# Graph-by-graph products in the hypergraph layer of a four-layer graph network, and attention masks on two row groups of the array

## The chip, the cores and the metric

The kernel runs on one core of a Trainium2 chip. The metric is the device time of one execution in microseconds (us), the median over several runs; lower is better.

## What is computed

128 graphs of 64 nodes with 256 features pass through four layers, each followed by a residual sum and a layer normalisation. The change touches the first (attention with masks) and the third (hypergraph convolution), cut here to what matters:

```
# layer 0, 8 heads of 64
dots = jnp.where(m2, einsum('bhid,bhjd->bhij', q, k) * scale, -big)      # m2: mask of row node and mask of column node
attn = softmax(dots) * LA + LG * adj + LD * jnp.exp(-dist)
# layer 2, twice (256 -> 512 with relu and a norm, then 512 -> 256)
H   = (adj != 0)                                   # 64 x 64 per graph
Dn  = 1 / einsum('nce,ne->nc', H, adj[:, 0])       # 0 where the sum is 0
Be  = 1 / H.sum(axis=1)
m   = Be[:, :, None] * einsum('nce,nch->neh', H, x @ W.T)
out = Dn[:, :, None] * einsum('nce,neh->nch', H, m) + b
```

With G = Dn H Be H^T the layer is G (x W^T) = (G x) W^T. G is a 64 x 64 matrix per graph.

## The kernel before

A group is eight graphs, 512 nodes, held as four tiles (T = 4) of 128 nodes: two graphs to a tile, nodes on the partitions. There are 16 groups. In each round of the main loop four streams work on four different groups: N (split and projections of the newest group), A (attention), B (the mean layer and the hypergraph layer) and D (the last layer). The order in which each engine walks through the steps of a round is a list written out by hand (`PE_ORDER`, `ACT_ORDER`, `DVE_ORDER`, `POOL_ORDER`); the change leaves the four lists as they are. Every engine works strictly through its list and waits on counting semaphores. The 16 groups overlap, so that the last groups run in rounds in which streams are missing.

PSUM has eight banks of 128 x 512 float32. Streams N and A use banks 0 to 3 in turn, B and D banks 4 to 7, so the bank of a step is given by its place in `PE_ORDER`; `filled` and `emptied` count when a bank is full and when its earlier reader is done. `apart` adds an increment of a semaphore that nobody waits for between two waits.

Steps that the text speaks of:

- `mixmat` and `score` (stream A). The mask of the node pairs is added by TensorE itself: a product of two small factors with 4 rows, `mi` (4 x 128 per tile) and `mj` (4 x 64 per tile), in bfloat16. `score` first writes it into the banks `s_even` and `s_odd` with four products of 256 columns (L1083), then adds 32 products of queries and keys on squares of 64 x 64 (L1093). There are two `score` steps in a round.
- `graph_c`: S = (H^T scaled by Be) times H^T into bank `sym`, four products 128 x 128 (L1182), float32. A tile holds two graphs, so H^T is two 64 x 64 squares on the diagonal and zeros elsewhere. VectorE multiplies the bank by `dn` into `gmat` (L890). `graph_d` transposes it (L1190) and ScalarE copies it to `gT`.
- `spread`: the feature gather G x, transposed: features on the partitions, nodes on the columns. Step 0 is features 0 to 127 into one bank, step 1 features 128 to 255 into the next, four products 128 x 128 each (L1201). ScalarE rounds each bank to `spT_hi` (L578), VectorE writes the rest to `spT_lo` (L709).
- `v` 2: six products of 512 columns for attention values, the step between `spread` 1 and `up` 0 in `PE_ORDER`.
- `up` 0 to 3: W1 times the gathered features, six products of 512 columns each (L1022 to L1024), the first three on feature chunk 0 and the next three on chunk 1.
- `pv` (L1128) fills two banks `oT` at once with 32 products on 64 x 64 squares; ScalarE copies both (L601), VectorE subtracts (L709), and `out0` (L1022, `wo_hi`) reads the result.
- `sim` (L1284): products of 128 rows and 64 columns. `stat` (L1248): four products with one moving column.

A float32 product appears in the trace as two passes, each with a weight load of its own; a product of `_hi`/`_lo` operands or of bfloat16 appears as one.

Of the kernel before, what the change touches and what calls it, by code (L numbers as in the profile page):

```python
# [12 lines left out]
ALU = mybir.AluOpType  # L13
ACT = mybir.ActivationFunctionType
# [18 lines left out]
HC = HID // P  # L33
NBIAS = D
EPS_LN = 1e-5
MIX = 0.33
# [100 lines left out]
def graph_layers(nc, x, x_t, adj, adj_t, adj_row0, mask_rows, wqkv, w_out, b_out, w_mean_t, w1_t, b1_c, gamma_c, beta_c, w2_t, b2,  # L137
                 wqk_t, bqk_c, wl_t, bl, wr_t, wd_r, bd_r, ident_c, ones3_c, mrow_c, out):
    with ExitStack() as ctx:
# [38 lines left out]
        warm = sb("warm", [P, T])  # L178
        mcst = sb("mcst", [4, 1 + P])

        masks = sb("masks", [4, T * (P + N)], U8)
        mi = sb("mi", [4, T, P], BF16)
        mj = sb("mj", [4, T, N], BF16)
        xTin = sb("xTin", [P, C, TOK])
# [98 lines left out]
        def count(sem, g, k, back=0):  # L283


            n = g * PER[sem] + (k - back * PER[sem])
            return (zero_ready, 6) if isinstance(n, int) and n <= 0 else (SEM[sem], n)

        def apart(eng, g):
# [259 lines left out]
        def _(act):  # L549
# [71 lines left out]
            def up(g, i):  # L621
                if isinstance(g, int) and g == 0 and i == 0:
                    act.wait_ge(bias_in, 16 * 8)
                copy_out(g, "up", i, r[:, i, :], "relu_ready", ACT.Relu, bias=b1c[:, i:i + 1])

            def hid_hi(g, i):
                act.wait_ge(*count("relu_ready", g, i + 1))
                if i == C:
                    apart(act, g)
                    act.wait_ge(*filled("qk", C - 1, g, 1))  # L630
                    apart(act, g)
                    act.wait_ge(*filled("y3", T - 1, g, 1))
                act.activation(hT[0][:, i, :], r[:, i, :], ACT.Copy).then_inc(SEM["hT_hi"], 1)  # L633
# [18 lines left out]
            def qk(g, i):  # L652
# [10 lines left out]
                "graph_d": lambda g, i: copy_out(g, "gT", 0, flat(gT[:, :, :]), "gT_ready"),  # L663
                "spread": lambda g, i: copy_out(g, "spread", i, spT[0][:, i, :], "spread_hi"),
                "hid_hi": hid_hi, "sq": sq, "mean_h": mean_h,
# [6 lines left out]
        def _(dve):  # L672
# [117 lines left out]
            def mask(g, i):  # L790

                dve.wait_ge(*count("mask_in", g, 16))
                dve.scalar_tensor_tensor(out=mi[:, :, :], in0=masks[:, 0:T * P].rearrange("p (t n) -> p t n", n=P),
                                         scalar=mcst[:, 0:1], in1=mcst[:, 1:1 + P].rearrange("p (a n) -> p a n", a=1)
                                         .broadcast_to([4, T, P]), op0=ALU.max, op1=ALU.mult)\
                   .then_inc(SEM["mask_rows"], 1)
                dve.tensor_scalar(flat(mj[:, :, :]), masks[:, T * P:T * (P + N)], mcst[:, 0:1], None,
                                  ALU.max).then_inc(SEM["mask_rows"], 1)
                if isinstance(g, int) and g == 0:
                    other_weights(0)  # L800
# [84 lines left out]
            def graph_c(g, i):  # L885

                dve.wait_ge(*filled("sym", 0, g))
                src = bank_of("sym", 0)
                dve.wait_ge(*count("dn_ready", g, 1))
                ins = dve.tensor_tensor(gmat[:, :, :], src[:, :].rearrange("p (t n) -> p t n", t=T),  # L890
                                        wide(dn[:, :], P), ALU.mult)
                ins.then_inc(SEM["g_ready"], 1)

            def agg(g, i):

                lo, hi = 2 * i, 2 * i + 2
                dve.wait_ge(*filled("agg", i, g))
                src = bank_of("agg", i)
                dve.wait_ge(*count("rdeg_ready", g, 1))
                for k in range(2):  # L900
                    ins = dve.scalar_tensor_tensor(out=xl[1][:, lo + k, :], in0=src[:, k * D:(k + 1) * D],
                                                   scalar=rdeg[:, lo + k:lo + k + 1], in1=xl[1][:, lo + k, :],
                                                   op0=ALU.mult, op1=ALU.add)
                ins.then_inc(SEM["agg_out"], 1)
                dve.wait_ge(*count("agg_out", g, i + 1))
                apart(dve, g)
                dve.wait_ge(*count("x1_ready", g, 2))

                ins = dve.scalar_tensor_tensor(out=flat(xl[1][:, lo:hi, :]), in0=flat(xl[1][:, lo:hi, :]), scalar=0.0,
                                               in1=flat(xl[0][:, lo:hi, :]), op0=ALU.max, op1=ALU.add)  # L910
                ins.then_inc(SEM["sum1_ready"], 1)
                dve.wait_ge(*count("sum1_ready", g, i + 1))
                norm(g, 1, xl[1], lo, hi)

            def hid_lo(g, i):
# [61 lines left out]
            def agg3(g, i):  # L977
# [29 lines left out]
                "turn1": low_chunk(x1T, "turn1", "turn1"),  # L1007
                "spread": low_chunk(spT, "spread", "spread"),
                "turn3": low_chunk(xgT, "turn3", "turn3"),
# [4 lines left out]
        def _(pe):  # L1014
# [19 lines left out]
            def mixmat(g, i):  # L1034
# [4 lines left out]
                for t in range(T):  # L1039
                    ins = pe.matmul(dst[:, t * N:(t + 1) * N], mi[:, t, :], mj[:, t, :],  # L1040
                                    start=True, stop=True)
# [28 lines left out]
            def score(g, i):  # L1070
# [9 lines left out]
                apart(pe, g)  # L1080
                for e in range(2):
                    for k in range(2):
                        pe.matmul(dst[e][:, k * HP * N:(k + 1) * HP * N], mi[:, 2 * i + k, :],  # L1083
                                  mj[:, 2 * i + k:2 * i + k + 1, :].broadcast_to([4, HP, N]),
                                  start=(k == 0), stop=False, skip_group_check=True)
# [91 lines left out]
            def graph_c(g, i):  # L1177
                pe.wait_ge(*count("bht_ready", g, 1))
                pe.wait_ge(*emptied("sym", 0, g))
                dst = bank_of("sym", 0)  # L1180
                for t in range(T):
                    ins = pe.matmul(dst[:, t * P:(t + 1) * P], hT0[:, t, :], bhT[:, t, :], start=True, stop=True)  # L1182
                now_full(ins, "sym", 0)

            def graph_d(g, i):
# [5 lines left out]
                now_full(ins, "gT", 0)  # L1191

            def gathered(name, g, i, src, mat, halves=None):


                pe.wait_ge(*emptied(name, i, g))
                dst = bank_of(name, i)
                for t in range(T):
                    if halves and i == 0 and t % 2 == 0:
                        pe.wait_ge(*count(halves, g, t // 2 + 1))  # L1200
                    ins = pe.matmul(dst[:, t * P:(t + 1) * P], src[:, t, i * P:(i + 1) * P], mat[:, t, :],  # L1201
                                    start=True, stop=True)
                now_full(ins, name, i)

# [17 lines left out]

            def spread(g, i):
                pe.wait_ge(*count("gT_ready", g, 1))
                gathered("spread", g, i, xl[1], gT, "x2_ready")

            def up(g, i):
                if isinstance(g, int) and g == 0 and i == 0:
# [4 lines left out]
                now_full(product(dst[:, :], [(chunk(w1, c, slice(i * P, (i + 1) * P)), chunk(spT, c)) for c in range(C)],  # L1233
                                 [count("spread_lo", g, c + 1) for c in range(C)]), "up", i)

# [113 lines left out]
```

## Time and profile before

| | |
|---|---|
| median of 3 runs | 1185.15 us (1184.29 to 1186.23) |
| the profiled execution: time, span | 1184.85 us, 1182.8 us |
| mean granted TensorE clock | 0.986 |
| busy share of the span | TensorE 95%, its weight loads 80%, VectorE 78%, ScalarE 50%, GpSimd 48% |
| bytes moved | 31 GB/s over the span |

The engines are named PE (TensorE), PEld (its weight loads, which overlap PE), DVE (VectorE), ACT (ScalarE), POOL (GpSimd). The table gives shares of the whole span. Start times of successive passes tell what a pass costs in a stream; the duration shown for one pass holds its latency too and overlaps the next.

### The profile page before, as it was taken

What the parts mean: (1) busy time and instruction counts of PE and PEld (TensorE: products, weight loads), DVE (VectorE), ACT (ScalarE), POOL (GpSimd) and SP (SyncE); (2) the same over time, 40 slices, a digit from 0 to 9 for tenths busy, and PEclk for the clock granted to TensorE, in tenths of its full rate; (3) what the DMA queues carried; (4) which work ended last, traced back from release to release, by engine and by line L of the source; (5) the groups of instructions that cost most, each with busy time, mean ns of one, the idle gap of its engine ahead of it and who ended that gap; (6) DMA issues with size and microseconds to landing.
All of it is one profiled execution on the core that took longest, in us unless ns stands there. A gap on an engine that the chain in (4) does not pass through costs nothing.

```text
span 1182.8 us, 29171 instructions
## 1 busy us (share of the span) xinstructions
PE 1127.0 (95%) x10416; PEld 951.4 (80%) x10416; DVE 919.8 (78%) x2223; ACT 595.7 (50%) x1266; POOL 572.5 (48%) x731
## 2 busy tenths in 40 slices
PE   5889999999999999999999999999999999999875
PEld 4768888888888888888888888888888888888763
DVE  6675887878788887878877788788778878777865
ACT  2536465454646445474544647454464645546331
POOL 2426356382644628264472735537273553826341
PEclk9899999999999999999999999999999999999897
DMA  7010102010010201001020100102001010100000
GB/s 233 24 28 1 46 3 67 1 48 21 22 44 0 67 0 44 22 22 44 0 67 0 43 24 22 44 0 67 0 23 44 18 49 0 42 8 28 2 23 18
DMA packets 52868, 37.22 MB, mean 31 GB/s; under 512 B 28182, under 2 KB 47707, under 8 KB 52827
## 3 DMA queue, kind: packets, MB, share of 16 engines
q1 hardware_dynamic: 51272, 35.09, 9.7%
q10 hardware_dynamic: 1554, 1.58, 0.5%
q8 instruction: 26, 0.43, 0.1%
q14 instruction: 16, 0.12, 0.0%
HBM read 28.27 MB, written 8.39 MB: 31 GB/s over the span
## 4 chain that ended last, share of the span: by engine, by line
PE 90%; DVE 5%; ACT 2%; POOL 1%; issue 1%; DMA 0%; SPq 0%; POOLq 0%; DVEq 0%; ACTq 0%
PE bank L1022 22%; PE bank L1024 21%; PE bank L1023 20%; PE bank L1093 3%; PE bank L1128 3%; PE bank L1163 2%; PE bank L1220 2%; PE bank L1201 2%; PE bank L1106 2%; PE bank L1294 2%; PE bank L1258 2%; DVE oT_lo L709 2%; PE bank L1083 1%; PE bank L1284 1%; PE bank L1248 1%; PE bank L1182 1%
## 5 line engine op out<-in xcount | busy, mean ns | idle before, releaser
L529 POOL TENSOR_TENSOR prob<-prob,srec 128x512 f32<-128x512 f32 x64 | 71.6, 1118 | 146.9 <-DVE srec L832 146.9
L467 POOL TENSOR_SCALAR var<-mv 128x2 f32<-128x2 f32 x128 | 29.0, 227 | 208.6 <-DVE mv L779 208.6
L786 DVE TENSOR_SCALAR x<-x,mv,rstd 128x256 f32<-128x256 f32 x256 | 119.0, 522 | 3.8 <-POOL rstd L470 3.3
L590 ACT ACTIVATE v<-bank 64x256 f32<-64x256 f32 x256 | 96.7, 378 | 17.7 <-PE bank L1024 15.4
L477 POOL TENSOR_TENSOR bhT<-hT,be 128x512 f32<-128x512 f32 x16 | 18.3, 1144 | 168.3 <-PE bank L1172 168.3
L775 DVE BATCH_NORM_STATS2 stats<-x 128x6 f32<-128x256 f32 x256 | 96.4, 418 | 4.4
L470 POOL TENSOR_TENSOR rstd<-var,negh 128x2 f32<-128x2 f32 x128 | 91.1, 712 | 10.7
L534 POOL TENSOR_TENSOR prob<-prob,mix 128x512 f32<-128x512 f32 x64 | 86.7, 1355 | 6.0 <-POOL prob L529 1.9
L918 DVE TENSOR_TENSOR hT_lo<-r,hT_hi 128x512 fp32r<-128x512 f32 x64 | 69.7, 1089 | 22.4 <-ACT hT_hi L633 22.2
L1022 PE MATMUL bank<-wo_hi,oT_hi 128*128 128x256 f32 x256 | 75.1, 293 | 8.9 <-DVE oT_lo L709 8.9
L1022 PE MATMUL bank<-w_hi,hT_hi 128*128 128x258 f32 x256 | 75.8, 296 | 2.7 <-DVE hT_lo L918 2.1
L578 ACT ACTIVATE qT<-bank 128x512 f32<-128x512 f32 x64 | 38.4, 599 | 78.6 <-PE bank L1024 78.6
L578 ACT ACTIVATE yl<-bank 128x256 f32<-128x256 f32 x64 | 24.6, 385 | 105.7 <-PE bank L1024 105.3
L578 ACT ACTIVATE kT<-bank 128x512 f32<-128x512 f32 x64 | 38.2, 598 | 78.6 <-PE bank L1024 78.6
L490 POOL TENSOR_TENSOR r<-r 128x512 f32<-128x512 f32 x48 | 67.1, 1398 | 21.4 <-ACT r L638 18.4
L1024 PE MATMUL bank<-wo_hi,oT_lo 128*128 128x256 f32 x256 | 73.7, 288 | 0.0
L1023 PE MATMUL bank<-wo_lo,oT_hi 128*128 128x256 f32 x256 | 73.4, 287 | 0.0
L1023 PE MATMUL bank<-w_lo,hT_hi 128*128 128x258 f32 x256 | 72.4, 283 | 0.0
L1024 PE MATMUL bank<-w_hi,hT_lo 128*128 128x258 f32 x256 | 72.1, 282 | 0.0
L1022 PE MATMUL bank<-xT_hi,wk_hi 128*128 128x512 f32 x128 | 56.6, 442 | 13.7 <-DVE wk_lo L689 13.1
L578 ACT ACTIVATE pT<-bank 128x512 f32<-128x512 f32 x64 | 34.7, 595 | 59.1 <-PE bank L1106 59.1
L839 DVE TENSOR_TENSOR x<-bank,xin 128x512 f32<-128x512 f32 x32 | 22.1, 691 | 51.0 <-PE bank L1024 51.0
(202 smaller groups left out, 3697.9 us busy)
## 6 DMA issues: line engine op xcount, KB each, us to landing
xTin<-in_x_t SPq DMA_DIRECT2D x32, 256.0 KB, 2.8
xin<-in_x SPq DMA_DIRECT2D x16, 512.0 KB, 3.7
out_x<-x SPq DMA_DIRECT2D x32, 256.0 KB
adjA<-in_adj SPq DMA_DIRECT2D x16, 128.0 KB, 2.5
adjB<-in_adj_t SPq DMA_DIRECT2D x32, 64.0 KB, 3.1
adjC<-in_adj_t SPq DMA_DIRECT2D x32, 64.0 KB, 2.3
r<-in_wqkv ACTq DMA_DIRECT2D x2, 512.0 KB, 4.1
x<-in_wqkv SPq DMA_DIRECT2D x1, 512.0 KB, 8.2
```

The source lines that it names most:

```text
L470: pool.tensor_tensor(rstd[layer][:, lo:hi], var[layer][:, lo:hi], negh[:, lo:hi], ALU.pow).then_inc(SEM[f"rstd{n}"], 1)
L490: pool.tensor_tensor(r[:, 0, :], r[:, 0, :], r[:, i, :], ALU.add).then_inc(SEM["sqsum"], 1)
L529: pool.tensor_tensor(rows_of(u), rows_of(u), srec[:, k, :].rearrange("p (h a) -> p h a", a=1) .broadcast_to([P, 2 * HP, N]), ALU.mult).the ...
L534: pool.tensor_tensor(u, u, mix[:, t:t + 2, :].rearrange("p t (a n) -> p t a n", a=1) .broadcast_to([P, 2, HP, N]), ALU.add).then_inc(SEM[" ...
L578: act.activation(dst, src[:, part], func, **kw).then_inc(SEM[ready], 1)
L590: ins = act.activation(v[e * N:(e + 1) * N, i, gr, :, :], src[gr * N:(gr + 1) * N, e], ACT.Copy)
L775: dve.bn_stats(stats[layer][:, t, :], src[:, t, :]).then_inc(SEM[f"stats{n}"], 1)
L786: ins = dve.tensor_scalar(x[:, t, :], x[:, t, :], mv[layer][:, t, 0:1], rstd[layer][:, t:t + 1], ALU.subtract, ALU.mult)
L918: dve.tensor_tensor(hT[1][:, i, :], r[:, i, :], hT[0][:, i, :].bitcast(F32), ALU.subtract).then_inc(SEM["hT_lo"], 1)
L1022: pe.matmul(out_ap, l[0], rr[0], start=(fresh and j == 0), stop=False, skip_group_check=not fresh)
L1023: pe.matmul(out_ap, l[0], rr[1], start=False, stop=False, skip_group_check=not fresh)
L1024: ins = pe.matmul(out_ap, l[1], rr[0], start=False, stop=(last and j == len(pairs) - 1), skip_group_check=not fresh)
```

## The change

It has four parts. `graph_c` computes the two 64 x 64 squares of each tile alone (8 products on diagonal squares in place of 4), and VectorE scales the two squares in two operations. `spread` becomes one step: for each tile and each half of the features one product per graph, with the 64 nodes of the graph as rows, 128 features as weights and 64 moving columns; graph 0 of a tile goes to one bank, graph 1 to the other (16 products in place of 8). Each bank now holds both feature halves of four graphs, so ScalarE and VectorE read it contiguously and write it to every second stretch of 64 columns (`graph_of`), and `up` waits for both `spread_lo` before its first product. In `score` the mask factors lie on partitions 0 to 3 and again on 64 to 67; the products for `s_even` use the first copy, those for `s_odd` the second, and they alternate. The mask arrays therefore have 68 rows (MR) instead of 4.

```diff
+MR = N + 4
-        mcst = sb("mcst", [4, 1 + P])
-        masks = sb("masks", [4, T * (P + N)], U8)
-        mi = sb("mi", [4, T, P], BF16)
-        mj = sb("mj", [4, T, N], BF16)
+        mcst = sb("mcst", [MR, 1 + P])
+        masks = sb("masks", [MR, T * (P + N)], U8)
+        mi = sb("mi", [MR, T, P], BF16)
+        mj = sb("mj", [MR, T, N], BF16)
...
+        def graph_of(ap, h):
+            return ap[:, :, :].rearrange("p c (t a n) -> p c t a n", a=2, n=N)[:, :, :, h, :]
...
+            def spread(g, h):
+                act.wait_ge(*filled("spread", h, g))
+                act.activation(graph_of(spT[0], h), bank_of("spread", h)[:, :].rearrange("p (c t n) -> p c t n", c=C, t=T),
+                               ACT.Copy).then_inc(SEM["spread_hi"], 1)
...
-                ins = dve.tensor_tensor(gmat[:, :, :], src[:, :].rearrange("p (t n) -> p t n", t=T),
-                                        wide(dn[:, :], P), ALU.mult)
+                for h in range(2):
+                    at = slice(h * N, (h + 1) * N)
+                    ins = dve.tensor_tensor(gmat[at, :, at], src[at, :, at], wide(dn[at, :], N), ALU.mult)
...
+            def spread(g, h):
+                dve.wait_ge(*count("spread_hi", g, h + 1))
+                dve.tensor_tensor(graph_of(spT[1], h), bank_of("spread", h)[:, :].rearrange("p (c t n) -> p c t n", c=C, t=T),
+                                  graph_of(spT[0], h).bitcast(F32), ALU.subtract).then_inc(SEM["spread_lo"], 1)
...
-                for e in range(2):
-                    for k in range(2):
-                        pe.matmul(dst[e][:, k * HP * N:(k + 1) * HP * N], mi[:, 2 * i + k, :],
-                                  mj[:, 2 * i + k:2 * i + k + 1, :].broadcast_to([4, HP, N]),
+                for k in range(2):
+                    for e in range(2):
+                        rows = slice(e * N, e * N + 4)
+                        pe.matmul(dst[e][:, k * HP * N:(k + 1) * HP * N], mi[rows, 2 * i + k, :],
+                                  mj[rows, 2 * i + k:2 * i + k + 1, :].broadcast_to([4, HP, N]),
...
+                apart(pe, g)
                 for t in range(T):
-                    ins = pe.matmul(dst[:, t * P:(t + 1) * P], hT0[:, t, :], bhT[:, t, :], start=True, stop=True)
+                    for h in range(2):
+                        at = slice(h * N, (h + 1) * N)
+                        ins = pe.matmul(dst[at, t * P + h * N:t * P + (h + 1) * N], hT0[at, t, at], bhT[at, t, at],
+                                        start=True, stop=True, skip_group_check=True)
...
             def spread(g, i):
+                if i:
+                    return
                 pe.wait_ge(*count("gT_ready", g, 1))
-                gathered("spread", g, i, xl[1], gT, "x2_ready")
+                for h in range(2):
+                    pe.wait_ge(*emptied("spread", h, g))
+                    apart(pe, g)
+                ins = [None, None]
+                for t in range(T):
+                    if t % 2 == 0:
+                        pe.wait_ge(*count("x2_ready", g, t // 2 + 1))
+                        apart(pe, g)
+                    for c in range(C):
+                        for h in range(2):
+                            rows = slice(h * N, (h + 1) * N)
+                            col = (c * T + t) * N
+                            ins[h] = pe.matmul(bank_of("spread", h)[:, col:col + N], xl[1][rows, t, c * P:(c + 1) * P],
+                                               gT[rows, t, rows], start=True, stop=True, skip_group_check=True)
+                for h in range(2):
+                    now_full(ins[h], "spread", h)
...
-                                 [count("spread_lo", g, c + 1) for c in range(C)]), "up", i)
+                                 [count("spread_lo", g, C) for c in range(C)]), "up", i)
```

Where instructions stand on TensorE, at the gather. `gT,x` are the passes of `spread`, `wv` those of `v` 2, `yl,adjC` the last of stream D ahead of it. Before:

```order
L1294 MATMUL bank<-yl,adjC 128x257 [waits y3_ready,sim_ready]
L1201 MATMUL bank<-gT,x 128x128 [waits x2_ready,agg3_out,gT_ready]
L1201 MATMUL bank<-gT,x 128x128
L1201 MATMUL bank<-gT,x 128x128 [waits x2_ready]
L1201 MATMUL bank<-gT,x 128x128
L1201 MATMUL bank<-gT,x 128x128 [waits gT_ready]
L1201 MATMUL bank<-gT,x 128x128 x3
L1022 MATMUL bank<-wv_hi,xT_hi 128x512 [waits shift_ready]
```

Now, down to the first product of `up`:

```order
L1320 MATMUL bank<-yl,adjC 128x257 [waits y3_ready,sim_ready]
L1248 MATMUL bank<-gT,x 128x64 [waits gT_ready,x2_ready,agg3_out]
L1248 MATMUL bank<-gT,x 128x64 x7
L1248 MATMUL bank<-gT,x 128x64 [waits x2_ready]
L1248 MATMUL bank<-gT,x 128x64 x7
L1038 MATMUL bank<-wv_hi,xT_hi 128x512 [waits shift_ready]
L1039 MATMUL bank<-wv_lo,xT_hi 128x512
L1040 MATMUL bank<-wv_hi,xT_lo 128x512
L1038 MATMUL bank<-spT_hi,w_hi 128x512 [waits spread_lo,agg3_out]
```

Nothing has changed places with a step of another stream: eight products of 128 columns are sixteen of 64, the second bank is asked for at the start instead of in the middle, and the six products of `v` 2 still stand between the gather and `up` 0.

On VectorE, at `graph_c` of group 0, in a round ahead of the loop (the row `hT<-bank,dn` is the scaling of `sym` into `gmat`; the rows around it belong to the mean layer). Before:

```order
L775 BN_STATS stats<-x 128x6 [waits sum1_ready]
L775 BN_STATS stats<-x 128x6
L779 BN_AGGR mv<-stats 128x2 [waits stats1] x2
L890 TENSOR_TENSOR hT<-bank,dn 128x512 [waits dn_ready,bank4_full]
L901 SCALAR_TENSOR_TENSOR x<-bank,rdeg,x 128x256 [waits rdeg_ready,bank5_full]
L901 SCALAR_TENSOR_TENSOR x<-bank,rdeg,x 128x256
```

Now:

```order
L785 BN_STATS stats<-x 128x6 [waits sum1_ready]
L785 BN_STATS stats<-x 128x6
L789 BN_AGGR mv<-stats 128x2 [waits stats1] x2
L902 TENSOR_TENSOR hT<-bank,dn 64x4x64 [waits dn_ready,bank4_full]
L902 TENSOR_TENSOR hT<-bank,dn 64x4x64
L912 SCALAR_TENSOR_TENSOR x<-bank,rdeg,x 128x256 [waits rdeg_ready,bank5_full]
L912 SCALAR_TENSOR_TENSOR x<-bank,rdeg,x 128x256
```

The one operation over 128 partitions has become two over 64 partitions and half the columns, at the same place and behind the same waits.

## Rows read from the trace of the kernel before

**Rows 1.** The page: the chain that ended last, shares by engine.

```profile
PE 90%; DVE 5%; ACT 2%; POOL 1%; issue 1%; DMA 0%; SPq 0%; POOLq 0%; DVEq 0%; ACTq 0%
```

**Rows 2.** Windows, one round: length, busy time by engine (instructions), clock, DMA.

```profile
core 0: us, PE busy (x) PEld busy (x) DVE busy (x) ACT busy (x) POOL busy (x), PEclk, DMA share, GB/s
503.09:572.90 69.81, 69.37 (x652) 58.72 (x650) 56.11 (x137) 37.08 (x79) 35.80 (x45) 1.00 0.09 28
```

**Rows 3.** Timeline, PE, gather to `up` 0: start, us, line, passes.

```profile
508.05 1.95 PE L1201 MATMUL bank<-gT,x 128*128 128x128 f32 x16
509.75 0.47 PE L1022 MATMUL bank<-wv_hi,xT_hi 128*128 128x512 f32 x1
...
511.21 0.39 PE L1022 MATMUL bank<-spT_hi,w_hi 128*128 128x512 f32 x1
```

**Rows 4.** Timeline, ACT, the two copies of the gather.

```profile
509.13 0.60 ACT L578 ACTIVATE spT_hi<-bank 128x512 fp32r<-128x512 f32 x1 [0.21 <-PE bank L1201]
510.03 0.60 ACT L578 ACTIVATE spT_hi<-bank 128x512 fp32r<-128x512 f32 x1 [0.30 <-PE bank L1201]
```

**Rows 5.** Timeline, DVE: second low part of the gather, later work.

```profile
510.66 0.69 DVE L709 TENSOR_TENSOR spT_lo<-bank,spT_hi 128x512 fp32r<-128x512 f32 x1 [0.20 <-ACT spT_hi L578]
...
511.76 0.48 DVE L987 SCALAR_TENSOR_TENSOR yr<-bank,simrec,yr 128x256 f32<-128x256 f32 x1
```

**Rows 6.** Timeline, PE, around `score` 1.

```profile
516.57 0.39 PE L1024 MATMUL bank<-spT_hi,w_lo 128*128 128x512 f32 x1
516.89 0.60 PE L1083 MATMUL bank<-mj,mi 4*128 4x256 bf16 x4
517.42 1.16 PE L1093 MATMUL bank<-kT,qT 64*64 64x64 f32 x64
518.52 0.50 PE L1022 MATMUL bank<-wv_hi,xT_hi 128*128 128x512 f32 x1
```

**Rows 7.** Timeline, PE: `graph_c` and `sim`, each with its successor.

```profile
561.24 1.05 PE L1182 MATMUL bank<-bhT,hT 128*128 128x128 f32 x8
562.12 1.03 PE L1220 MATMUL bank<-r,adjB 128*128 128x256 f32 x4
...
567.51 1.15 PE L1284 MATMUL bank<-r 128*64 128x64 f32 x32
568.59 0.50 PE L1022 MATMUL bank<-wv_hi,xT_hi 128*128 128x512 f32 x1
```

**Rows 8.** Timeline, PE: `stat`, products with one moving column.

```profile
523.02 1.02 PE L1248 MATMUL bank<-one,r 128*128 128x1 f32 x8
523.91 1.07 PE L1106 MATMUL bank<-ident,prob 128*128 128x128 f32 x8
```

**Rows 9.** Lines by form, weight loads: busy us, mean ns, idle before.

```profile
L1201 PEld LDWEIGHTS bank<-gT,x 128*128 128x128 f32 x256 | 30.9, 191 | 2.4 <-ACT gT L578 1.7
...
L1284 PEld LDWEIGHTS bank<-r 128*64 128x64 f32 x512 | 16.2, 138 | 1.7 <-issue 0.4 <-DVE r L937 0.4
...
L1083 PEld LDWEIGHTS bank<-mj,mi 4*128 4x128 bf16 x128 | 9.4, 92 | 14.2 <-issue 13.1
...
L1172 PEld LDWEIGHTS bank<-row0p,bhT 128*128 128x128 bf16 x64 | 2.6, 97 | 4.4 <-issue 4.4
```

**Rows 10.** Timeline, PE: first `down` 3 product behind `pv` 0, first `out0` product.

```profile
527.45 0.39 PE L1022 MATMUL bank<-w_hi,hT_hi 128*128 128x258 f32 x1
...
529.53 0.39 PE L1022 MATMUL bank<-wo_hi,oT_hi 128*128 128x256 f32 x1 [0.37 <-DVE oT_lo L709]
```

**Rows 11.** Timeline, ACT: both copies behind that `pv`.

```profile
527.55 1.09 ACT L601 ACTIVATE oT_hi<-bank 128x512 fp32r<-128x512 f32 x2 [0.46 <-PE bank L1128]
```

**Rows 12.** Timeline, PE: gather and `up` 0 of the last group.

```profile
1127.85 2.02 PE L1201 MATMUL bank<-gT,x 128*128 128x128 f32 x16
1130.98 0.47 PE L1022 MATMUL bank<-spT_hi,w_hi 128*128 128x512 f32 x1 [1.11 <-DVE spT_lo L709]
```

**Rows 13.** Lines by form, DVE: reading a whole bank, and a diagonal half.

```profile
L969 DVE TENSOR_TENSOR adjC<-bank,adjC 64x256 f32<-64x256 f32 x32 | 13.3, 417 | 0.5 <-PE bank L1284 0.3
...
L890 DVE TENSOR_TENSOR hT<-bank,dn 128x512 f32<-128x512 f32 x16 | 11.0, 690 | 13.2 <-PE bank L1182 13.2
```

More of the change, by code:

```diff
@@ L663, in _ @@
                 "graph_d": lambda g, i: copy_out(g, "gT", 0, flat(gT[:, :, :]), "gT_ready"),
-                "spread": lambda g, i: copy_out(g, "spread", i, spT[0][:, i, :], "spread_hi"),
+                "spread": spread,
                 "hid_hi": hid_hi, "sq": sq, "mean_h": mean_h,
@@ L794, in mask @@
                                          scalar=mcst[:, 0:1], in1=mcst[:, 1:1 + P].rearrange("p (a n) -> p a n", a=1)
-                                         .broadcast_to([4, T, P]), op0=ALU.max, op1=ALU.mult)\
+                                         .broadcast_to([MR, T, P]), op0=ALU.max, op1=ALU.mult)\
                    .then_inc(SEM["mask_rows"], 1)
@@ L887, in graph_c @@
                 dve.wait_ge(*filled("sym", 0, g))
-                src = bank_of("sym", 0)
+                src = bank_of("sym", 0)[:, :].rearrange("p (t n) -> p t n", t=T)
                 dve.wait_ge(*count("dn_ready", g, 1))
-                ins = dve.tensor_tensor(gmat[:, :, :], src[:, :].rearrange("p (t n) -> p t n", t=T),
-                                        wide(dn[:, :], P), ALU.mult)
+                for h in range(2):
+                    at = slice(h * N, (h + 1) * N)
+                    ins = dve.tensor_tensor(gmat[at, :, at], src[at, :, at], wide(dn[at, :], N), ALU.mult)
                 ins.then_inc(SEM["g_ready"], 1)
@@ L1007, in _ @@
                 "turn1": low_chunk(x1T, "turn1", "turn1"),
-                "spread": low_chunk(spT, "spread", "spread"),
+                "spread": spread,
                 "turn3": low_chunk(xgT, "turn3", "turn3"),
@@ L1039, in mixmat @@
                 for t in range(T):
-                    ins = pe.matmul(dst[:, t * N:(t + 1) * N], mi[:, t, :], mj[:, t, :],
+                    ins = pe.matmul(dst[:, t * N:(t + 1) * N], mi[0:4, t, :], mj[0:4, t, :],
                                     start=True, stop=True)
@@ L1191, in graph_d @@
                 now_full(ins, "gT", 0)
[L1193 to L1203, printed above, removed]
             def y1(g, i):
@@ L1323, with twice @@
     mrow[2:4, 1 + N:] = [[-BIG], [BIG]]
+    def twice(rows):
+        both = _np.zeros((MR,) + rows.shape[1:], rows.dtype)
+        both[0:4], both[N:N + 4] = rows, rows
+        return both
     m = a["nodemask"]
@@ L1329 @@
         "x": a["x"], "x_t": a["x"].reshape(B * N, D).T, "adj": a["adj"], "adj_t": _np.swapaxes(a["adj"], 1, 2),
-        "adj_row0": a["adj"][:, 0, :].reshape(B // 2, P).T, "mask_rows": _np.concatenate([rows, cols], axis=2).reshape(4, -1),
+        "adj_row0": a["adj"][:, 0, :].reshape(B // 2, P).T, "mask_rows": twice(_np.concatenate([rows, cols], axis=2).reshape(4, -1)),
         "wqkv": _np.moveaxis(a["L0_gnn_W_qkv"].reshape(D, H, 3, DH), 2, 0).reshape(3, D, H * DH), "w_out": a["L0_gnn_W_out"].reshape(HP, 2, DH, D)[_np.arange(HP)[:, None], _np.array([[0, 1], [1, 0]] * (HP // 2))].reshape(HID, D), "b_out": a["L0_gnn_b_out"],
@@ L1336 @@
         "wr_t": a["L3_gnn_Wr"].T, "wd_r": a["L3_gnn_Wd"].reshape(D), "bd_r": a["L3_gnn_bd"],
-        "ident_c": ident, "ones3_c": ones3, "mrow_c": mrow,
+        "ident_c": ident, "ones3_c": ones3, "mrow_c": twice(mrow),
     }
```

## The prediction

> **What bounds the kernel.** I read the page's chain first: the reader is to see that TensorE alone carries 90% of it [rows 1]. Then the windows of one round of the main loop: TensorE is busy 69.37 of 69.81 us, at full granted clock, while VectorE and ScalarE have 14 and 33 us to spare [rows 2]. So a round costs what TensorE's list costs, plus the few places where it waits, and a microsecond taken from or put into that list counts 16 times, once for each group. The timeline then gives prices. I take them from start to start of successive runs of passes, never from a single duration, since those overlap. What has to be found is what the new small products cost in such a stream, and whether `up` 0 still finds its input ready.
>
> **The masks in `score`.** Four products of 256 columns stand between 516.89 and 517.42, 0.53 us [rows 6]. 256 columns at the full clock of 2.4 GHz are 0.107 us, four are 0.43, and 0.10 is the change over to the squares of the scores. Ahead of them lies another 0.09: the product before starts at 516.57 and lasts 0.23 in its stream (511.21 − 509.75 holds six of them and one change). With the two copies of the factors on different row groups, each pair can run at once. That rows 0 to 63 and 64 to 127 can work together is seen in the scores themselves: 64 passes in 1.10 us, 17 ns each [rows 6], where the passes of `sim`, which use all rows and two column halves, take (568.59 − 567.51)/32 = 34 ns [rows 7]. Twice as many tiles, half the time. So 0.21 us is saved in each `score`, **0.42 in a round**. The bounds are 0 (pairs one after another; nothing in this trace writes full-width bfloat16 results to two banks at once) and 0.42. I take 0.42, since it is the nearest form.
>
> **`graph_c`.** Eight passes take 562.12 − 561.24 = 0.88 us [rows 7]. Afterwards there are sixteen passes on the two diagonal squares. In `sim` two tiles make 34 ns per pass, so a tile does one pass in 68 ns; the scores give the same, 4 x 17. Hence 16 x 0.034 = 0.54, with 0.10 for the change into squares and perhaps 0.05 on the way out: 0.69, **0.19 saved**. Bounds: 0 and 0.34 (no changeover). On VectorE one operation of 690 ns becomes two of 417 [rows 13], 0.14 us more, on an engine with 14 us to spare, and its bank is full 0.19 sooner; `graph_d` comes 13 us later on TensorE.
>
> **The gather itself.** Sixteen passes take 509.75 − 508.05 = 1.70 us, 106 ns each, which is 128 columns twice over the clock [rows 3]. The new passes move 64 columns, half of that, in two row groups at once: sixteen for each group of rows. Going by moving columns the gather should shrink to 32 x 34 ns = 1.09. But each pass first needs its weights, and these are still 128 columns. `stat` shows what such a load costs by itself: eight passes with a single moving column take 523.91 − 523.02 = 0.89 us, 111 ns each [rows 8]. And the columns set the load, not the rows: 191 ns for 128 float32 columns against 138 for 64, a difference of 53, while 4 rows of 128 bfloat16 columns take 92 and 128 rows take 97 [rows 9]. So a row group cannot begin a pass oftener than every 111 ns: 16 x 0.111 = 1.78 us. If the 12 to 15 ns by which a small tile's pass (68) exceeds its 53 ns of columns comes on top, it is 16 x 0.123 = 1.97. I take the middle, 1.87, and add 0.10 for going over to row groups and 0.03 for the way back (the product behind squares lasts 0.50, that behind the gather 0.47 [rows 3, 6]). That makes 2.00, **0.30 more than now**. Bounds: 1.22 and 3.6 (the loads of the two row groups one after another, 32 x 0.111); the scores' 17 ns per load and pass speak against the latter.
>
> The Trainium skill pulls two ways here. Its page "TensorEngine Tiling (Array Packing)", section "Theoretical Speedup", gives up to 2x where a dimension is at most 64, which by this row's 1.70 would be 0.85 us for the gather. Its page "TensorE: Matmul & The Clock Gate", section "LDWEIGHTS (loading the stationary operand)", has the load go by the columns of the weights and not by their rows, 128/1.2 = 107 ns, which would be 1.71. By that second rule, the trace agrees (111 ns [rows 8]); no pass of this form is in the trace.
>
> **The relay behind the gather.** This is the term that I trust most. Today bank 0 is full in the middle of the gather: ScalarE copies it from 509.13 and the second from 510.03, VectorE's second half starts at 510.66 and ends at 511.35 [rows 4, 5], and `up` 0, which starts at 511.21 [rows 3], needs only the first half for its first three products. Now both banks fill with the last pass, two copies and two subtractions stand behind each other, and the first product of `up` waits for all. The trace holds exactly this relay: `pv` fills two banks together, ScalarE copies both in 1.09 us [rows 11], VectorE subtracts both, and `out0` can start 529.53 − 527.45 = 2.08 us after TensorE went on to other work [rows 10]. Behind the gather the other work is `v` 2, 1.46 us [rows 3], 1.48 after squares. **TensorE then waits 0.60 us.** Bounds 0.45 and 0.78 (if ScalarE starts 0.28 after the gather's end, as in rows 4, and not 0.10). The wait would be shown as some 0.4, as the 2.08 shows 0.37, since the shown duration of the last pass covers the rest. The output in stretches of 64 columns I cost at nothing; if it made both engines slower, the wait would grow by as much. Behind the relay on VectorE stands the last of stream D's sums, whose bank `up` 1 needs: today it ends at 512.24 [rows 5], 0.89 after the relay; then some 2.9 us after the gather, and `up` 1 comes at 2.08 + 1.4 = 3.5, so it isn't late.
>
> **The last group** has no `v` 2 between. It gathers from 1127.85 and starts `up` at 1130.98 [rows 12], 3.13 later. The new figure is the gather as now, 1.75, plus 2.08 = 3.83, so 0.70 more.
>
> **At nothing**: 68 mask rows instead of 4 (some 50 KB more in a round in which DMA is 9% busy [rows 2], asked for a round ahead), VectorE's mask operations (as many elements per partition as before), and five more unwaited increments on TensorE in a round. If these cost something, the 0.09 ahead of the masks, where three stand [rows 6], is the ceiling: 0.15 in a round.
>
> **Sum.** In each of 16 groups −0.42 − 0.19 + 0.30 = −0.31, makes −5.0. The wait in 15 groups is +9.0, the last group +0.7. Total +4.7, so the profiled 1184.85 becomes 1189.6; it lies 0.3 below the median of before, so 1189.7.
>
> **The rivals.**
> 1. *The gather at the pace of small tiles.* Loads hide behind moving columns: 1.22 instead of 2.00, −0.78 x 16 = −12.5, time 1177. For it: the scores and `sim`, whose loads hide. Against: their loads have 64 columns, and `stat` costs 111 ns with nothing to move. It decides as soon as a pass in a row group takes under 105 ns. 0.20. The halving in "Theoretical Speedup" of the Trainium skill's page "TensorEngine Tiling (Array Packing)" would be this way.
> 2. *The relay is covered.* If the two copies and subtractions ended within `v` 2, +9.0 falls away: 1180.6. For it only that today's wait there is nil; against, 2.08. 0.08.
> 3. *The mask pairs don't overlap.* +6.7: 1196.4. For it: no such pair in the trace. 0.12.
> 4. *Loads of the two row groups one after another.* 3.6 + 0.13 for the gather, +1.73 x 16 = +28: 1217. Against: 17 ns per load in the scores. 0.04.
> 5. *My forecast*, 1189.7, its own range 1186.5 to 1194 from the bounds of load pace (±0.10 x 16) and wait (−2.3, +2.7). 0.56.
>
> **How the numbers follow.** A measurement of this kernel tells about 0.2%, 2.4 us, from no change. Faster come rivals 1 and 2, 0.28. Within 0.2% falls the lowest part of the forecast and a mixture of 1 with 3: 0.14. Slower is the rest, 0.58. The range takes in rivals 1 to 3 and leaves out 4: 1176 to 1198.
>
> **What would show it.** The passes `gT,x` from first start to the start of `v` 2: 1.9 to 2.1 us if the loads bind, 1.2 if I am wrong. Idle before the first `spT_hi` product of about 0.4, released by `spT_lo`, in every round. `mj,mi` to `kT,qT`: 0.32 instead of 0.53. `bhT,hT` to its successor 0.7 instead of 0.88. The round: 70.1 instead of 69.81 us. The prediction is wrong if the gather's passes come at 34 ns, or if the relay, for any reason, takes under 1.6 us.

## The result, and the profile after

The changed kernel takes 1200.41 us (median of 4 runs, 1199.42 to 1201.81) against 1185.01 for the kernel before on the same chip: a ratio of 1.013, 95% interval 1.0112 to 1.0147. It is slower by 15.4 us, where 4.7 were predicted. The profiled execution has a span of 1200.0 us, 17.2 more than before.

Timeline of TensorE around the gather of the same round, then `graph_c` (start, us, line, form, passes):

```profile
513.39 1.03 PE L1320 MATMUL bank<-yl,adjC 128*128 128x257 f32 x4
514.35 2.00 PE L1248 MATMUL bank<-gT,x 64*128 64x64 f32 x32
516.28 0.50 PE L1038 MATMUL bank<-wv_hi,xT_hi 128*128 128x512 f32 x1
...
518.45 0.47 PE L1038 MATMUL bank<-spT_hi,w_hi 128*128 128x512 f32 x1 [0.52 <-DVE spT_lo L928]
...
524.22 0.39 PE L1100 MATMUL bank<-mj,mi 4*128 4x256 bf16 x4
524.54 1.16 PE L1110 MATMUL bank<-kT,qT 64*64 64x64 f32 x64
...
530.34 1.02 PE L1274 MATMUL bank<-one,r 128*128 128x1 f32 x8 [0.16 <-POOL r L495]
...
568.30 0.40 PE L1040 MATMUL bank<-hT_hi,wqk_lo 128*128 128x512 f32 x1
568.63 0.68 PE L1202 MATMUL bank<-bhT,hT 64*64 64x64 f32 x16
569.24 1.13 PE L1229 MATMUL bank<-r,adjB 128*128 128x256 f32 x4
```

Beside [rows 3]: the gather lasts 516.28 − 514.35 = 1.93 us instead of 1.70, and it starts 0.96 behind the product ahead of it (0.87 before). The first `up` product starts 2.17 after the gather's end instead of 1.46. In between stand ScalarE's two copies and VectorE's two subtractions, here called the relay, in the timelines of the two engines:

```profile
516.38 1.09 ACT L633 ACTIVATE spT_hi<-bank 128x512 fp32r<-128x512 f32 x2 [1.25 <-PE bank L1248]
```

```profile
517.01 1.29 DVE L928 TENSOR_TENSOR spT_lo<-bank,spT_hi 128x512 fp32r<-128x512 f32 x2 [1.18 <-ACT spT_hi L633]
```

Beside [rows 6]: the masks take 524.54 − 524.22 = 0.32 instead of 0.53. Beside [rows 7]: the squares take 0.61 instead of 0.88, but they start 0.10 late, and the four passes behind them take 0.78 where they took 0.68. And there is a wait that nobody asked about: `stat`, released by GpSimd.

The windows show how these pieces stand in a round. Of the kernel before, from its gather: gather, gather to `up`, `up` to `stat`, `stat` to the next `k` product.

```profile
508.05:509.75 1.70, 1.70 (x18) 1.70 (x16) 1.33 (x7) 1.45 (x4) 0.76 (x2) 1.00 0.00 0
509.75:511.21 1.46, 1.46 (x9) 1.21 (x8) 1.24 (x2) 0.60 (x1) 0.17 (x1) 1.00 0.00 0
511.21:523.02 11.81, 11.81 (x123) 9.72 (x122) 10.35 (x19) 9.26 (x18) 7.34 (x6) 1.00 0.00 0
523.02:537.02 14.00, 13.56 (x211) 12.13 (x211) 9.20 (x26) 7.91 (x18) 11.99 (x21) 1.00 0.15 47
```

The same four of the changed kernel:

```profile
514.35:516.28 1.93, 1.93 (x33) 1.86 (x32) 1.24 (x6) 0.77 (x3) 0.92 (x2) 1.00 0.00 0
516.28:518.45 2.17, 1.65 (x9) 1.08 (x7) 1.40 (x4) 1.56 (x4) 0.00 (x0) 1.00 0.00 0
518.45:530.34 11.89, 11.73 (x122) 9.62 (x123) 9.40 (x17) 9.10 (x18) 7.36 (x6) 1.00 0.00 0
530.34:544.32 13.98, 13.55 (x210) 12.13 (x211) 9.19 (x26) 7.79 (x18) 11.97 (x21) 1.00 0.15 47
```

The third line is the one to look at. Between `up` and `stat` lie the masks of `score` 1, which are 0.21 us shorter, and yet the stretch is 0.08 longer. The page of the changed kernel has it as well: the chain that ended last is no longer TensorE's alone.

```profile
PE 67%; issue 10%; POOL 10%; DVE 8%; ACT 5%; DMA 0%; POOLq 0%; SPq 0%; DVEq 0%; ACTq 0%
```

From here on a "round" is a tenth of the time between the starts of the 4th and the 14th gather of a profile. It is 69.79 us before and 70.58 after, so 0.79 a round, where the sum had 0.29. The 17.2 us of the two profiles are 1.97 ahead of the first gather (91.78 instead of 89.81), 11.76 between the first gather and the last, and 3.46 from the last on. Windows of before, last gather to `stat` and from there to the end of TensorE's work:

```profile
1127.85:1142.79 14.94, 11.27 (x65) 9.39 (x65) 9.27 (x22) 8.67 (x16) 5.07 (x6) 1.00 0.00 1
1142.79:1172.69 29.90, 21.77 (x125) 16.97 (x125) 14.91 (x40) 5.61 (x12) 10.91 (x20) 0.83 0.07 22
```

And after:

```profile
1141.58:1159.44 17.86, 13.74 (x81) 11.74 (x81) 9.36 (x22) 8.39 (x15) 5.42 (x7) 0.84 0.00 1
1159.44:1189.88 30.44, 22.32 (x125) 17.46 (x125) 14.91 (x40) 5.77 (x13) 10.57 (x19) 0.82 0.07 22
```

The first stretch grew by 2.92 us. 0.94 of it is the gather with its relay, 4.07 instead of 3.13 [rows 12]. The other 1.98 lie between `up` and `stat`, 13.79 instead of 11.81, where the granted clock averages 0.79 instead of 1.00: TensorE ran at 1.2 GHz for part of it. The window of that stretch alone:

```profile
1145.65:1159.44 13.79, 11.74 (x49) 9.85 (x49) 5.68 (x11) 7.30 (x13) 4.50 (x5) 0.79 0.00 1
```

### The profile page after: what moved, and what is told of

Same layout as the page of the kernel before. It is cut to its first block, busy times and chain, and to the rows that moved or that the text cites. A ratio compares the mean times of both kernels' runs of the same rounds, so it can differ in the third digit from the quotient of the medians.

```text
span 1200.0 us, 29979 instructions
## 1 busy us (share of the span) xinstructions
PE 1132.2 (94%) x10800; PEld 941.3 (78%) x10800; DVE 914.3 (76%) x2239; ACT 597.1 (50%) x1266; POOL 572.5 (48%) x731
## 4 chain that ended last, share of the span: by engine, by line
PE 67%; issue 10%; POOL 10%; DVE 8%; ACT 5%; DMA 0%; POOLq 0%; SPq 0%; DVEq 0%; ACTq 0%
PE bank L1038 17%; PE bank L1040 15%; PE bank L1039 15%; POOL r L495 5%; PE bank L1145 3%; PE bank L1229 3%; PE bank L1180 2%; PE bank L1123 2%; PE bank L1284 2%; ACT v L595 2%; DVE oT_lo L719 2%; POOL prob L539 2%; PE bank L1110 1%; PE bank L1310 1%; POOL prob L534 1%
## 5 line engine op out<-in xcount | busy, mean ns | idle before, releaser
L475 POOL TENSOR_TENSOR rstd<-var,negh 128x2 f32<-128x2 f32 x128 | 91.2, 712 | 10.7
L934 DVE TENSOR_TENSOR hT_lo<-r,hT_hi 128x512 fp32r<-128x512 f32 x64 | 59.7, 933 | 40.3 <-ACT hT_hi L643 40.3
L1038 PE MATMUL bank<-spT_hi,w_hi 128*128 128x512 f32 x128 | 52.3, 409 | 9.9 <-DVE spT_lo L928 9.9
```

The source lines that it names most:

```text
L475: pool.tensor_tensor(rstd[layer][:, lo:hi], var[layer][:, lo:hi], negh[:, lo:hi], ALU.pow).then_inc(SEM[f"rstd{n}"], 1)
L934: dve.tensor_tensor(hT[1][:, i, :], r[:, i, :], hT[0][:, i, :].bitcast(F32), ALU.subtract).then_inc(SEM["hT_lo"], 1)
L1038: pe.matmul(out_ap, l[0], rr[0], start=(fresh and j == 0), stop=False, skip_group_check=not fresh)
```

## The experiments

Twelve kernels; each ratio is against the kernel before, measured beside it. First the parts one by one, from the kernel before.

**masks_only.** The mask factors twice, `s_even` and `s_odd` on different rows, nothing else of the change.

```diff
-                for e in range(2):
-                    for k in range(2):
-                        pe.matmul(dst[e][...], mi[:, 2 * i + k, :], mj[:, ...]
+                for k in range(2):
+                    for e in range(2):
+                        rows = slice(e * N, e * N + 4)
+                        pe.matmul(dst[e][...], mi[rows, 2 * i + k, :], mj[rows, ...]
```

> The kernel before with the mask factors on two row groups and nothing else. Theory 1: between the start of the first up product and stat a chain over ScalarE, VectorE and GpSimd sets the end (11.8 us in both traces, TensorE waits 0.13 for it before and 0.32 after), so that what score 1 saves there is waited away again at stat; only score 0 counts: a round shorter by 0.21 us, 3.4 us in all, about 1181.6. Theory 2: both scores count, 0.42 a round, 6.7 us, about 1178.3.

Measured: 1182.04 us, ratio 0.998 (0.9968 to 0.9991). The round is 69.55 us, 0.24 less; `up` to `stat` is 11.80 as before. Theory 1 holds: one of the two savings counts.

**masks_second.** The same, but only in `score` 1.

```diff
-                        rows = slice(e * N, e * N + 4)
+                        rows = slice(e * N, e * N + 4) if i == 1 else slice(0, 4)
```

> As masks_only, but only score 1 (the one between up and stat) uses the second row group. Theory 1: the product runs of the masks take 0.32 instead of 0.53 us, stat starts as long after up as before, and the round is as long as before (69.8 us): about 1185. Theory 2: a round shorter by 0.21, 3.4 us, about 1181.6.

Measured: 1185.40 us, ratio 1.0001 (0.9991 to 1.0011), a round of 69.76. Its timeline of TensorE:

```profile
517.46 0.39 PE L1085 MATMUL bank<-mj,mi 4*128 4x256 bf16 x4
517.78 1.16 PE L1095 MATMUL bank<-kT,qT 64*64 64x64 f32 x64
523.59 1.02 PE L1250 MATMUL bank<-one,r 128*128 128x1 f32 x8 [0.17 <-POOL r L491]
```

The masks take 0.32 us here too, and TensorE waits that much longer for `r` at `stat`. This saving is worth nothing: `stat` starts when GpSimd has finished the three sums of squares that it reads, and these start behind ScalarE. GpSimd in the kernel before, then in masks_second:

```profile
518.50 4.37 POOL L490 TENSOR_TENSOR r<-r 128x512 f32<-128x512 f32 x3 [0.47 <-ACT r L638]
```

```profile
519.08 4.37 POOL L491 TENSOR_TENSOR r<-r 128x512 f32<-128x512 f32 x3 [0.47 <-ACT r L639]
```

The sums end at 522.87 and 523.45, and `stat` starts 0.15 and 0.14 behind them (523.02 [rows 8] and 523.59). So `stat` waits for GpSimd in the kernel before already.

**squares_only.** `graph_c` on diagonal squares, both its products and VectorE's two operations.

```diff
-                    ins = pe.matmul(dst[:, t * P:(t + 1) * P], hT0[:, t, :], bhT[:, t, :], start=True, stop=True)
+                    for h in range(2):
+                        at = slice(h * N, (h + 1) * N)
+                        ins = pe.matmul(dst[at, t * P + h * N:t * P + (h + 1) * N], hT0[at, t, at], bhT[at, t, at], ...)
```

> The kernel before with graph_c on diagonal squares alone. Theory 1 (the sum goes by what TensorE's list costs): 0.17 us less in a round, 2.8 us, about 1182.3. Theory 2 (small tiles bring a longer stretch at half clock at the start, 2 us of it seen before the first gather with all parts together): up to 2 us of this is lost, about 1184.

Measured: 1183.92 us, ratio 0.9988 (0.9979 to 0.9998), a round of 69.68: 0.11 less. Not the 0.17 of theory 1: the passes save 0.27 (0.61 instead of 0.88), going into the squares costs 0.10 and coming back another 0.10. That leaves 0.07; the other 0.04 of the round isn't accounted for. In sixteen rounds 0.11 makes 1.8 us, and the medians differ by 1.4, so the 2 us of theory 2 aren't seen in them. In this profile the first gather begins at 92.45 us instead of 89.81. Over the profiles here that start varies between 89.8 and 93.2 without order between kernels, so I don't put the 2 us of the changed kernel's start down to its parts.

**gather_only.** The gather as one step into two banks, with `up` waiting for both halves; masks and `graph_c` as before. The edit is the part of the change's diff that concerns `spread` and `up`.

> The kernel before with the gather as one step into two banks, masks and graph_c as before. Theory 1: 0.32 us for the gather's passes, 0.74 for the wait before up and its restart, nothing of it recovered: a round longer by 1.06, 16 us, and 2 to 4 us at both ends: 1203 to 1205. Theory 2 (part of the extra time of the changed kernel comes from the other two parts): under 1200.

Measured: 1204.60 us, ratio 1.0161 (1.0145 to 1.0178), a round of 70.88: 1.09 more, within 0.03 of theory 1. The whole loss and more is here.

**masks_squares.** The other two parts together, with the old gather.

> The kernel before with the row-group masks and the diagonal squares, the gather as it was. Theory 1: 0.24 and 0.11 us of a round add, a round of 69.44, about 1180.5, which would put the cost of the new gather in the changed kernel at 20 us. Theory 2 (the two parts interact): 1183 or more.

Measured: 1179.35 us, ratio 0.9943 (0.9926 to 0.9959), a round of 69.48. The parts add (0.24 + 0.11 = 0.35 predicted, 0.31 measured). So the new gather costs the changed kernel 1200.4 − 1179.4 = 21 us (22 by the two ratios). `score` 0 and `graph_c` both stand between `k` and the next gather; that is where a saving on TensorE counted.

Then the two costs of the gather, on the changed kernel.

**gather_64.** Each product cut into two of 64 feature columns, which uses all four squares of the array; twice the passes.

```diff
-                            ins[h] = pe.matmul(bank_of("spread", h)[:, col:col + N], xl[1][rows, t, c * P:(c + 1) * P],
+                                ins[h] = pe.matmul(bank_of("spread", h)[to, col:col + N],
+                                                   xl[1][rows, t, c * P + f * N:c * P + (f + 1) * N],
                                                gT[rows, t, rows], start=True, stop=True, skip_group_check=True)
```

> The changed kernel, but each gather product is cut into two of 64 feature columns, so that its weights have 64 columns instead of 128 and four squares of the array are used; twice as many passes, 64. Theory 1 (a row group cannot begin a pass before its 128 columns of weights are loaded): passes at 17 ns, the gather's length 1.1 instead of 1.93 us, a round 0.8 shorter, about 1187. Theory 2 (the passes cost what they cost by number, or by switching between row groups): 64 passes take as long as 32 or longer, 1200 or more.

Measured: 1186.95 us, ratio 1.0017 (1.0005 to 1.0029), a round of 69.74. Its ten runs spread from 1185.11 to 1190.88, and the profile is of the fastest. Its timeline:

```profile
508.02 1.16 PE L1249 MATMUL bank<-gT,x 64*64 64x64 f32 x64
509.11 0.50 PE L1038 MATMUL bank<-wv_hi,xT_hi 128*128 128x512 f32 x1
...
511.30 0.47 PE L1038 MATMUL bank<-spT_hi,w_hi 128*128 128x512 f32 x1 [0.54 <-DVE spT_lo L928]
```

64 passes take 1.09 us, where 32 took 1.93. Each square does sixteen passes of 64 moving columns, as each row group did, in 4 x 17 = 68 ns instead of 121; what is halved is the width of the weights and of the tile. Its weight loads by form, and those of the changed kernel (busy us, mean ns):

```profile
L1249 PEld LDWEIGHTS bank<-gT,x 64*64 64x64 f32 x1024 | 16.4, 134 | 6.5 <-issue 4.7 <-ACT gT L583 1.8
```

```profile
L1248 PEld LDWEIGHTS bank<-gT,x 64*128 64x128 f32 x512 | 29.9, 188 | 6.5 <-issue 4.7 <-ACT gT L583 1.8
```

A load of 64 rows and 128 columns lasts 188 ns, that of 128 rows 191 [rows 9]; halving the columns takes 54 off it, halving the rows 3. The Trainium skill's page "TensorE: Matmul & The Clock Gate", section "LDWEIGHTS (loading the stationary operand)", has the load go by columns alone; the trace agrees. The changed gather goes at 1.93/16 = 121 ns for each pass of a row group, 10 above the 111 that `stat` shows for such a load with one moving column, and halving the columns brought it down: so the load is what bounds it. The 10 ns aren't explained. The wait in front of `up` stays as it was, 2.19 us after the gather.

**hi_first.** In `up` the four products that read only `spT_hi` come first, so that the subtraction is off the path of the first product.

```diff
+                pe.wait_ge(*count("spread_hi", g, C))
+                for c in range(C):
+                    pe.matmul(dst[:, :], w[c][0], s[c][0], start=(c == 0), stop=False)
+                    pe.matmul(dst[:, :], w[c][1], s[c][0], start=False, stop=False)
+                pe.wait_ge(*count("spread_lo", g, C))
+                for c in range(C):
+                    ins = pe.matmul(dst[:, :], w[c][0], s[c][1], start=False, stop=(c == C - 1))
```

> The changed kernel, but up adds its six products in another order: first the four that read only spT_hi, behind both copies, then the two that read spT_lo. Nothing else moves. Theory 1 (the relay costs what it shows): up starts 1.5 us after the gather's end instead of 2.16, its restart of 0.08 goes too, a round of 69.8 us instead of 70.58, in all some 12 us less: 1188. Theory 2 (a later wait in the same chain takes its place, at the subtraction or at stat): over 1195.

Measured: 1190.93 us, ratio 1.0043 (1.0026 to 1.006), a round of 70.12. `up` starts 1.49 after the gather, as theory 1 has it, but 0.24 of the 0.67 is given back: `up` to `stat` is 12.13 instead of 11.89. Theory 2 is right in kind. Where to look is `up` 1; VectorE, then TensorE of this kernel:

```profile
514.19 0.48 DVE L1003 SCALAR_TENSOR_TENSOR yr<-bank,simrec,yr 128x256 f32<-128x256 f32 x1
```

```profile
514.18 0.63 PE L1266 MATMUL bank<-spT_lo,w_hi 128*128 128x512 f32 x2
514.73 0.51 PE L1262 MATMUL bank<-spT_hi,w_hi 128*128 128x512 f32 x1
515.08 0.40 PE L1263 MATMUL bank<-spT_hi,w_lo 128*128 128x512 f32 x1
```

`up` 1 could begin at 514.18 + 2 x 0.23 = 514.65. Its bank is held by the last sum of stream D, which VectorE reaches only behind the relay and ends at 514.67. `up` 1 starts at 514.73, and its first product holds 0.35 instead of 0.23: 0.20 lost together. The profile shows no idle time there, since the last pass's duration covers it.

**gather_64_hi.** Both edits.

> Both edits together on the changed kernel. Theory 1: the two add, a round of 69.0 us, about 1175. Theory 2 (with the faster gather something else behind it becomes late, the bank reads or the last sum of stream D): the gains overlap, 1180 or more.

Measured: 1178.29 us, ratio 0.9942 (0.9923 to 0.9961), a round of 69.32 with 12.16 from `up` to `stat`. Faster than both kernels, but by 0.3 us less per round than theory 1, for the same reason as in hi_first. It is level with masks_squares.

The last four test that reason, and what else waits.

**hi_first_soft.** On hi_first, VectorE does `soft` 1 while it waits for ScalarE's first copy, not behind the relay.

```diff
-    ("D", "agg3", 2), ("B", "spread", 0), ("B", "spread", 1), ("D", "agg3", 3), ("A", "soft", 1), ("B", "hid_lo", 0),
+    ("D", "agg3", 2), ("A", "soft", 1), ("B", "spread", 0), ("B", "spread", 1), ("D", "agg3", 3), ("B", "hid_lo", 0),
```

> hi_first with one step moved in VectorE's list: soft 1 (a sum over 512 elements and a reciprocal, 0.85 us) stands ahead of the two subtractions of the gather, where VectorE waits 1.2 us for ScalarE, instead of behind the last sum of stream D. Theory 1 (in hi_first the relay's lateness goes on through VectorE's queue to the low parts of the hidden layer and to stat, up to stat 12.13 instead of 11.8 us): up to stat is 11.8 or less, a round of 69.8 or less instead of 70.12, 5 us or more off the 1190.9. Theory 2 (the 0.33 comes from the other order of up's passes): no change, 1190.

Measured: 1189.78 us, ratio 1.0032 (1.0019 to 1.0044), a round of 70.00 and 12.00 from `up` to `stat`. Neither theory: of the 0.33 the move takes 0.13, and 11.81 + 0.20 = 12.01 is what the late `up` 1 leaves. The 0.13 lie in GpSimd's three sums. They start 7.49 us after `up` 0 in hi_first and 7.48 here, but last 4.50 instead of 4.36 (the row here is in the last section). In hi_first:

```profile
520.74 4.50 POOL L495 TENSOR_TENSOR r<-r 128x512 f32<-128x512 f32 x3 [0.27 <-ACT r L648]
```

In hi_first VectorE's later subtractions `hT_lo` stand nearer to these sums and last 1.42 and 1.51 us, here 0.69 and 1.37. The move also brought GpSimd's two steps on `prob` forward (512.03 instead of 517.41). That the sums are longer because of the subtractions beside them fits the last section; no run separates it. The median moves by 1.1 us only.

**g64_hi_soft.** The same move on gather_64_hi.

> The same move on the kernel with the 64-column gather and the reordered up. Theory 1: up to stat 11.8 or less instead of 12.16, a round of 68.9 instead of 69.3, about 1172. Theory 2: no change, 1178.

Measured: 1178.90 us, ratio 0.9944 (0.9928 to 0.9961), a round of 69.50: worse by 0.17 than without the move, with 12.34 from `up` to `stat`. With the short gather VectorE has only 0.35 us of idle time ahead of the relay, and `soft` 1 takes 0.85. So the relay and the release of the bank come later, and `up` 1 starts 0.89 after the last two passes of `up` 0 began, where it was 0.56. Timeline of TensorE:

```profile
509.89 0.50 PE L1255 MATMUL bank<-spT_hi,w_hi 128*128 128x512 f32 x1 [0.16 <-DVE yr L994]
```

Of these 0.33 the shorter sums on GpSimd (4.36 instead of 4.52) give 0.16 back.

**g64_hi_soft_out0** and **ms_out0.** `out0` in the order of `up` above, on g64_hi_soft and on masks_squares. In both the sums of `out0` that reach the output are not those of the layer; passes, sizes and waits are as intended, and only the times are used.

```diff
-                pe.wait_ge(*count("oT_lo", g, 2 * i + 2))
+                pe.wait_ge(*count("oT_hi", g, 2 * i + 2))
                 pe.wait_ge(*emptied("out0", i, g))
...
+                pe.wait_ge(*count("oT_lo", g, 2 * i + 2))
```

> The kernel before this one in the list, and out0 adds the products that read only oT_hi first, as up does. Theory 1: the wait of 0.53 us before out0 (the relay behind pv) goes too, a round of 68.4, about 1164. Theory 2 (steps behind out0 are bound by VectorE's subtraction all the same): under 2 us gained.

> The kernel before with the row-group masks, the diagonal squares and out0 reordered; gather and up as before. Theory 1: 0.53 us a round off the 69.48, 8 us, about 1171. Theory 2: under 2 us, 1178.

Measured: 1177.65 us and a round of 69.54 for the first, against 1178.90 and 69.50; 1181.29 us (seven runs, 1177.65 to 1184.32) and 69.48 for the second, against 1179.35 and 69.48. Nothing gained in a round, theory 2, but for another reason than it names. Timelines of GpSimd and TensorE in ms_out0:

```profile
535.04 2.52 POOL L523 TENSOR_TENSOR xT_lo<-xTin,xT_hi 128x512 fp32r<-128x512 f32 x2
```

```profile
537.69 0.49 PE L1024 MATMUL bank<-xT_hi,wk_hi 128*128 128x512 f32 x1 [0.49 <-POOL xT_lo L523]
```

The half microsecond turns up again ahead of `k`, which waits for the low part that GpSimd makes: its end at 537.56, `k` 0.13 behind it. It is the same in the kernel before, where `k` starts at 537.02:

```profile
534.37 2.52 POOL L522 TENSOR_TENSOR xT_lo<-xTin,xT_hi 128x512 fp32r<-128x512 f32 x2
```

Its end is 536.89, and `k` follows 0.13 behind. GpSimd is busy 11.99 of the 14.00 us between `stat` and `k` there (fourth line of the windows above), and what is idle are waits for its own and `stat`'s results.

## Why the prediction was wrong

Its direction was right, its size a third of what was measured, and the time lies outside the range. The forecast is missed by 10.7 us: (0.79 − 0.29) x 16 = 8.0 in the rounds, and the rest lies outside them. By its own steps, per round:

| term | predicted | measured | shown by |
|---|---|---|---|
| masks, `score` 0 | −0.21 | −0.21 | masks_only less masks_second |
| masks, `score` 1 | −0.21 | −0.03 | masks_second |
| `graph_c` | −0.19 | −0.11 | squares_only |
| gather | +0.30 | +0.32 | profile after |
| relay | +0.60 | +0.78 | profile after, gather_only |
| sum | +0.29 | +0.75 (the round: +0.79) | |

- **The step that failed in kind** is "what the kernel is bound by": "a microsecond taken from or put into that list counts 16 times". It held for what was put in ahead of `up`, but of what is taken out only for `score` 0 and, mis-sized, `graph_c`, between `k` and the next gather. `up` to `stat` is 11.80 to 11.81 us in the five kernels with the old gather and `out0`, whatever `score` 1 does; there a chain over the other engines sets the end, and 0.18 of the 0.21 expected is waited away. In the trace of before this wait was hidden: `stat` starts 0.25 after the product ahead of it where 0.12 is the pace, and no idle time is shown. Of the same kind is `stat` to `k`, which ate the saving at `out0`.
- **Mis-sized terms.** The relay was 2.17 us, not 2.08 (0.09), and the product behind a wait holds 0.31 instead of 0.23 (0.08). The rule that a wait costs exactly its length was wrong by this restart. Copies and subtractions take as long as in the relay behind `pv` (1.09 and 1.29), so the stretches of 64 columns cost nothing, as predicted; the 0.09 lies between VectorE's end (518.30) and the first product of `up` (518.45), and its cause is open. `graph_c` comes to −0.11: its sixteen passes take 0.61, not 0.54, and the way back to float32 products costs 0.10, not 0.05.
- **What held**: the load of 128 columns as the bound of the new gather (2.00 predicted with the change to row groups, 2.02 measured: 1.93 and 0.09), the overlap of the mask pairs (0.32), the relay as the main loss, and the bank of `up` 1 being no problem as long as `up` itself is late. Rivals 1 to 4 all fell. The rival missing from the list was one in which a saving is made and then waited away; rival 3 doubted only that it is made. In the forecast's own range the lower end should be 1185.8 by the bounds it names (1189.7 − 1.6 − 2.3), not 1186.5.
- **The ends.** For the gather and relay of the last group the sum held 0.30 + 0.70 = 1.00; 0.94 was measured. The lower clock behind it, some 2 us, it didn't have. What brought the clock down isn't shown, and a longer idle time ahead of `up` can't be all of it. In the last group of hi_first and of hi_first_soft the gather with the wait behind it takes 3.24 and 3.23 us, close to the 3.13 of before. These are their stretches from `up` to `stat`, hi_first first:

```profile
1135.77:1147.73 11.96, 9.41 (x49) 7.48 (x49) 6.36 (x14) 7.48 (x14) 4.15 (x4) 1.00 0.00 1
```

```profile
1133.62:1147.54 13.92, 11.86 (x49) 9.96 (x49) 6.48 (x14) 7.30 (x13) 4.63 (x5) 0.78 0.00 0
```

One kept the full clock, the other lost 2 us like the changed kernel. The 2 us at the start of the profile are within the scatter of profiles. The medians differ by less than the profiled executions (15.4 against 17.2 in span), so how much the ends cost in the other runs isn't known.

## What to carry to other kernels

A product with 64 moving columns, split by rows over the array, didn't get cheaper while its weights kept their 128 columns: the row group still waits for the load. Split the columns too (64 passes in 1.09 us against 32 in 1.93). Filling two banks together instead of one after the other puts copies and subtractions in one row; look for the same relay elsewhere in the trace and compare it with the work that stands between. And before counting a saving on the busiest engine, measure the stretch from the last step that others wait for to the next step that waits for others: if a second chain fills it, the saving is worth nothing, even if the profile shows no idle time there.

## What the runs showed of the hardware

VectorE's subtraction `hT_lo`, with both operands in SBUF (the on-chip memory), can last twice as long while GpSimd works. In hi_first_soft, VectorE, then GpSimd:

```profile
517.62 0.69 DVE L925 TENSOR_TENSOR hT_lo<-r,hT_hi 128x512 fp32r<-128x512 f32 x1 [0.72 <-ACT hT_hi L634]
...
521.01 1.37 DVE L925 TENSOR_TENSOR hT_lo<-r,hT_hi 128x512 fp32r<-128x512 f32 x1 [0.92 <-ACT hT_hi L634]
```

```profile
520.53 4.36 POOL L486 TENSOR_TENSOR r<-r 128x512 f32<-128x512 f32 x3 [6.08 <-ACT r L639]
```

0.69 us with GpSimd idle, 1.37 when it starts behind the first of GpSimd's three sums. The one that starts first isn't lengthened in this row of the kernel before, where the subtraction is 0.16 ahead of GpSimd (VectorE, then GpSimd):

```profile
514.81 0.64 DVE L918 TENSOR_TENSOR hT_lo<-r,hT_hi 128x512 fp32r<-128x512 f32 x1
```

```profile
514.97 1.38 POOL L529 TENSOR_TENSOR prob<-prob,srec 128x512 f32<-128x512 f32 x1 [5.05 <-DVE srec L832]
```

The order of GpSimd's steps is therefore part of VectorE's cost, and an edit that moves one against the other can move this too.
